# One core, macaron block with routed experts: scatters and q reads moved within the attention turn, settling merged into attention, expert weights fetched before rows

## What is computed

```python
x = x + 0.5 * ffn(_layernorm(x), waff, W1, b1, W2, b2, thr)
x = x + attn(_layernorm(x), W_qkv, u_qkv, sigma_qkv, W_proj, u_proj, sigma_proj)
x = x + 0.5 * ffn(_layernorm(x), waff, W1, b1, W2, b2, thr)
# ffn: aff = (x @ waff.T) / (|x| |waff| + 1e-9); every token goes to its best of 8 experts,
#      if its rank in its batch for that expert is < cap, where
#      cap = clip(floor(S * sigmoid(aff.mean() - thr)), 4, S); other tokens enter as zero
#      h = gelu(xi @ W1e + b1e); out += h @ W2e + b2e            (D=128, F=512, E=8)
# attn: 16 heads of 8, qkv = x @ (sigma_param / sigma * W_qkv), causal softmax, then W_proj
```

## Time and profile before

| | |
|---|---|
| runs before | 1085.56 us median of 3 (1085.16 to 1087.98) |
| profiled execution | 1081.78 us, span 1080.0 us, mean granted PE clock 0.942 |
| PE, VectorE, ACT, GpSimd busy | 904.3, 712.7, 595.9, 721.9 us |
| DMA packets | 127407, 89.72 MB, mean 83 GB/s |

### The profile page before, as it was taken

How to read it: one execution, slowest core, us unless ns; L and a number is a source line. 1 busy time by engine, 2 the same in 40 slices (tenths; PEclk the granted TensorE clock), 3 DMA queues, 4 the chain that set the end, 5 groups by cost and what they waited for, 6 DMA issues and landing times. The chain is left out here.

```text
span 1080.0 us, 26507 instructions
## 1 busy us (share of the span) xinstructions
PE 904.3 (84%) x8184; PEld 688.8 (64%) x8217; DVE 712.7 (66%) x2348; ACT 595.9 (55%) x1547; POOL 721.9 (67%) x1328
## 2 busy tenths in 40 slices
PE   5846479999747898989899999989998872899995
PEld 4733379999724555556556565556555551899995
DVE  7979734444227777878888888888888744444441
ACT  2434156666414665656666666666666550666663
POOL 6619768644035678878888898888887773255554
PEclk9999679999959999999999999999999995899998
DMA  7450022223135544354454535454544201222220
GB/s 197 121 176 0 4 60 68 68 66 66 41 86 107 106 90 98 94 98 100 97 105 96 117 96 107 100 101 96 100 107 96 53 23 38 63 68 63 66 64 20
DMA packets 127407, 89.72 MB, mean 83 GB/s; under 512 B 14305, under 2 KB 117910, under 8 KB 127270
## 3 DMA queue, kind: packets, MB, share of 16 engines
q1 hardware_dynamic: 103078, 52.69, 21.6%
q10 hardware_dynamic: 15488, 17.74, 8.1%
q0 software_dynamic: 8704, 17.60, 6.0%
HBM read 52.23 MB, written 35.47 MB: 81 GB/s over the span
## 5 line engine op out<-in xcount | busy, mean ns | idle before, releaser
L1250 ACT ACTIVATE at_pt<-at_pm 128x512 f32<-128x512 f32 x384 | 228.9, 597 | 158.9 <-PE at_pm L1336 91.7
L1558 DVE TENSOR_REDUCE at_mx<-at_pp 128x2 f32<-128x512 f32 (+1 forms) x384 | 261.7, 683 | 81.4 <-PE at_pp L1325 45.7
L1157 POOL TENSOR_SCALAR_AFFINE_SELECT at_pt<-at_pt 128x256 f32<-128x256 f32 (+1 forms) x384 | 185.7, 489 | 65.6 <-ACT at_pt L1250 61.8
L904 ACT ACTIVATE e_ht<-e_ps_h,b1t 128x128 f32<-128x128 f32 x576 | 165.0, 370 | 92.7 <-PE e_ps_h L932 92.4
L932 PE MATMUL e_ps_h<-e_xnt,e_w1own 128*128 128x128 f32 x1152 | 157.1, 281 | 3.7 <-DVE e_w1own L983 3.7
L942 PE MATMUL e_ps_y<-w,e_ht 128*128 x1152 | 159.2, 282 | 0.0
L932 PEld LDWEIGHTS e_ps_h<-e_xnt,e_w1own 128*128 128x128 f32 x1152 | 144.9, 198 | 4.2 <-issue 2.9
L942 PEld LDWEIGHTS e_ps_y<-w,e_ht 128*128 128x128 f32 x1152 | 140.0, 192 | 1.7
L989 DVE SCALAR_TENSOR_TENSOR e_y<-e_ps_y,e_x 128x256 f32<-128x256 f32 x72 | 30.6, 425 | 161.9 <-PE e_ps_y L942 161.9
L870 POOL DMA_INDIRECT out_dram<-e_y,e_x x72 | 73.9, 1027 | 93.3 <-DVE e_y L989 81.7
L1323 PE MATMUL at_pp<-kb,qs 96*128 96x512 bf16 x256 | 99.4, 388 | 14.1 <-DVE at_mx L1558 13.3
(11 more groups left out here) (322 smaller groups left out, 1776.9 us busy)
## 6 DMA issues: line engine op xcount, KB each, us to landing
at_qkd<-at_part SPq DMA_DIRECT2D x64, 192.0 KB, 2.8
kb<-at_qkd SPq DMA_DIRECT2D x64, 96.0 KB
qs<-at_qkd ACTq DMA_DIRECT2D x64, 96.0 KB
e_x<-buckets SPq DMA_DIRECT2D x72, 66.0 KB, 1.9
x<-e_y SPq DMA_DIRECT2D x36, 128.0 KB, 1.8
rows<-ts_x ACTq DMA_DIRECT2D x16, 264.0 KB, 2.8
ts_x<-in_x_dram SPq DMA_DIRECT2D x16, 256.0 KB, 3.9
x_by_token<-at_xa SPq DMA_DIRECT2D x32, 128.0 KB
```

Source lines behind the costliest of these rows:

```text
L904: last = a.activation(hid_t[j % NB][:, f, :], ps_h[j % NB][:, f, :], ACT.Gelu, bias=c.b1t[:, ds(e, 1), f])
L1157: g.affine_select(out=tile, in_=tile, compare_op=ALU.is_ge, fill=0.0, base=0, pattern=[[0, n], [1, P]], channel_multiplier=-1).then_inc(ma ...
L1250: a.activation(pt[u % RING][:, :], pm[u % 2], ACT.Exp, scale=SCALE).then_inc(exped, 1)
L1558: v.tensor_reduce(out, src, axis=AX.X, op=ALU.max).then_inc(maxed, 1)
```

## The change

In attention, the two scatters move from steps 4 and 6 to 7 and 9, the three pairs of q reads from steps 10, 11 and 1 of the next turn to 9, 10 and 11, and the gathers take their indices from `place` itself. The section `settle` becomes the end of attention's streams, with the same operations, in PSUM that attention already has. In both expert sections ACT runs a Gelu on one element first, and VectorE copies the first four weights before it waits for rows.

```diff
@@ experts
+            a.activation(early[0:1, 0:1], c.part[0:1, 0:1], ACT.Gelu).then_inc(early_done, 1)
             for i in range(-TURN, NU):
@@
             dve.wait_ge(c.w1_in, 16)
+            e = experts_of(dve, 0)
+            for j in range(FETCH):
+                fetch(j, e[j])
             for i in range(-NORM, NU):
                 if i + NORM < NU:
                     keep(i + NORM)
                 for j in (2 * i, 2 * i + 1):
-                    if 0 <= j + FETCH < NS:
+                    if FETCH <= j + FETCH < NS:
@@ attention, SP
             run(turn)
             sp.wait_ge(blanked, 16)
+            sp.wait_ge(tail_done, 1)
+            blank_tails(sp, 0)
+            sp.wait_ge(tailed, 16 * E)
             for k in range(NQ):
                 sp.wait_ge(row_out[k], 32 * (B // NQ))
@@ attention, GpSimd
+            pool.wait_ge(zeroed, NZ)
@@
-                    if u == 0 and has(4):
-                        wait(pool, xa_in[k % 2], xa_count(b + 2)(k))
-                        g.tensor_copy(index[k % 2][:, :], c.place[:, ds((b + 4) * TPB, TPB)]).then_inc(index_done, 1)
@@
-                            wait(pool, index_done, n + 1)
                         pool.indirect_dma_start(xa[k % 2][:, j, 0:D], None, x_dram,
-                                                bass.IndirectOffsetOnAxis(ap=index[k % 2][:, j:j + 1], axis=0)).then_inc(xa_in[k % 2], 16)
+                                                bass.IndirectOffsetOnAxis(ap=c.place[:, n * TPB + j:n * TPB + j + 1], axis=0)).then_inc(xa_in[k % 2], 16)
@@
-                    if u in (4, 6) and has(-4):
-                        n, j = b - 4, (u - 4) // 2
+                    if u in (7, 9) and has(-4):
+                        n, j = b - 4, (u - 7) // 2
@@ attention, ACT
-                    if u == 1 and has(2):
-                        q_rows(b + 2, (k + 2) % NQ, k % 2, 2)
@@
-                    if u in (10, 11) and has(3):
-                        q_rows(b + 3, (k + 3) % NQ, (k + 1) % 2, u - 10)
+                    if u in (9, 10, 11) and has(3):
+                        q_rows(b + 3, (k + 3) % NQ, (k + 1) % 2, u - 9)
             run(turn)
+            act.wait_ge(tail_done, 1)
+            blank_tails(act, HALF)
+            act.wait_ge(e_ask, 1)
+            a.activation(cell[:, 2:3], cell[:, 1:2], ACT.Exp, scale=-1.0).then_inc(e_got, 1)
@@ attention, PE: behind run(turn), settle's matmuls, the first of them after
+            pe.wait_ge(seen, TPB * B)
@@ attention, VectorE: behind run(turn), settle's chain, after
+            dve.wait_ge(summed, B)
```

More of the change, by code:

```diff
@@ L805, in experts @@
         y_out = [sem(f"yout{k}") for k in range(NR)]
-        fills = sem("fills")
+        fills, early_done = sem("fills"), sem("early")
+        early = t.sb(f"{tag}_early", [1, 1])
         xn_done, x_tr, x_tr_out, up, gelu, down, y_done, w1_done, kept = (
@@ L1062, in attention @@
         kept = [sem(f"kept{k}") for k in range(2)]
-        index_done = sem("index")
-        index = two("index", [P, TPB], I32)
         size, wnorm_d, tiny, far = two("size", [P, TPB]), sb("wnorm_d", [P, E]), sb("tiny", [P, TPB, E]), sb("far", [P, TPB, E], BF16)
@@ L1080, in attention, with blank_tails @@
         NM = 5
-        blk = ctx.enter_context(nc.Block())
+        cell, cols = sb("cell", [P, 8]), sb("cols", [P, 2])
+        count, tiles, tile_end, jump, ended, skipped = (sb(n, [P, E]) for n in ("count", "tiles", "end", "jump", "ended", "skipped"))
+        tail_f, tail = sb("tail_f", [1, E]), sb("tail", [1, E], I32)
+        ps_n, ps_sum, ps_row = pp[0][:, 0:E], pp[1][:, 0:1], pm[0][:, 0:2 * P]
+        settled, counted, sum_ask, sum_got, e_ask, e_got, table, rowed, tail_done, tailed = (
+            sem(n) for n in "settled counted sum_ask sum_got e_ask e_got table rowed tail tailed".split())
+        HALF = E // 2
+        blk = ctx.enter_context(nc.Block())
+        def blank_tails(eng, first):
+            _, row = nc.values_load_multi_w_load_instructions(
+                tail[0:1, first:first + HALF], engines=[eng.engine], min_val=0, max_val=E * STRIDE - P,
+                skip_runtime_bounds_check_because="a bucket of STRIDE rows holds at most T tokens, so its end leaves P rows of it")
+            for e in range(HALF):
+                eng.dma_start(io["buckets"][ds(row[e], P), :], c.blank[:, :]).then_inc(tailed, 16)
         x_t = nc.dram_tensor("x1_by_token", (T, D), F32, kind="Internal").ap()
@@ L1456, in _ @@
             run(turn)
+            pe.wait_ge(seen, TPB * B)
+            te.matmul(ps_n, c.onesb[:, :], c.hots[B % 2][:, 3 * TPB, :], start=True, stop=True).then_inc(counted, 1)
+            pe.wait_ge(sum_ask, 1)
+            te.matmul(ps_sum, c.ones[:, :], cell[:, 0:1], start=True, stop=True).then_inc(sum_got, 1)
+            pe.wait_ge(table, 1)
+            for i in range(2):
+                last = te.matmul(ps_row[0:1, i * P:(i + 1) * P], cols[:, i:i + 1], c.ident[:, :], start=True, stop=True)
+            last.then_inc(rowed, 1)
         @blk.vector
@@ L1612, in _ @@
             run(turn)
[L1615 to L1666, removed]
@@ L1667, in _ @@
+            s = Steps(dve, settled)
+            dve.wait_ge(summed, B)
             v.tensor_reduce(cell[:, 0:1], c.aff_sum[:, :, :], axis=AX.XY, op=ALU.add).then_inc(sum_ask, 1)
@@ L1683, in _ @@
             dve.wait_ge(sum_got, 1)
-            v.scalar_tensor_tensor(cell[:, 1:2], ps_sum[:, 0:1], 1.0 / (T * E), c.thr[:, :], ALU.mult, ALU.subtract).then_inc(e_ask, 1)
+            v.scalar_tensor_tensor(cell[:, 1:2], ps_sum, 1.0 / (T * E), c.thr[:, :], ALU.mult, ALU.subtract).then_inc(e_ask, 1)
             dve.wait_ge(rowed, 1)
@@ L1707, in macaron @@
         attention(nc, m, io, c, x1)
-        settle(nc, m, io, c)
         experts(nc, m, io, c, "e2", out, False)
```

## The result

The changed kernel takes 1061.03 us (median; 1059.28 to 1062.2) against 1085.57 beside it (1085.16 to 1087.98): ratio 0.977, 95% interval 0.9743 to 0.9798. That is 24.5 us where 30.5 were forecast (1085.5 to 1055). The profiled execution takes 1060.11, span 1058.4, 21.6 less than the span of before.

A forecast was written before the change was run, and what follows sets the result against it. PE was taken to set attention's pace, interrupted by late transfers. From 1081.8 us, attention 19, settling 5.9 and weights 2.6 and 1.0 (28.5) gave 1053.3, plus 1.9 gave 1055; own range 1047 to 1062, whole range 1044 to 1070.

The forecast's parts named there:

- Rival B: Attention reads stay bound by the DMA engines and k becomes the last; gain there only 5.6 us, 1068.6 total; chance 0.26.
- D: Attention: ACT waits in step 9 for landed parts, 1.54 us a turn, 37 over 24 turns; 1092 us, slower; chance 0.05.
- q's rows, 16 + 4.8: Attention: earlier q reads take 1.1 us off each PE wait, 16 in all, plus 4.8 from three low-clock turns.
- The subtraction one microsecond earlier: Attention: without step 4's scatter ahead of it, GpSimd's part subtraction L1212 goes about 1.0 us earlier, and so the parts land.
- New waits, -2: Attention: loss of 1 us for GpSimd's bunched work and 1 for waits showing once PE no longer pauses.
- rival C: Attention: GpSimd's new order delays masks and L1181, ACT waits in step 11; 10 of the 19 us lost, 1065; chance 0.13.
- Index copies, 0: GpSimd in attention: dropping one 0.18 us copy per turn gains nothing, as PE hides it; upper bound 5.8 us.
- Settling, 5.9: End of attention: with settling merged, the second experts' first load goes at 910.3 instead of 916.3, 5.9 us gained; bounds 3.5 to 7.0.
- Weights ahead of rows, 2.6 and 1.0: Experts sections: first expansion starts 2.6 us earlier in the first, 1.0 in the second, and the lead lasts.
- Early Gelu: Experts sections: moving a 1.28 us table load earlier gains nothing; up to 1.3 each if ACT were the limit.
- The added 1.9: Added to the sum: half of the 3.8 us by which the profiled execution lay below the median of the runs.

The follow-up runs named there:

- the kernel with gathers held: Changed kernel with the last four of the first 16 gathers in the first experts section held back for the first two blocks' results; 1048.31 us, ratio 0.9747 to before.

## Why the prediction came out as it did

- **Time and class.** 1061 lies inside the range and inside the forecast's own; 6 us less were saved than forecast. That it is not further off is in part luck: attention gave 5.7 us more than forecast and the first experts 8.7 less. Rival B (1068.6) asked for waits on `kb`; they fell from 3.9 to 1.5. D (1092) asked for ACT to be held in steps 9 and 10; the changed kernel's first profile shows no such wait. Its second has 2 turns, 5.6 us, and PE waits 1.2 and 1.5 us right behind them. D's step is real and rare, not in every turn.
- **q's rows, 16 + 4.8.** Forecast 19 for attention, measured 24.7 between the two profiles, 23.2 between the means of three kernels with the old attention (531.5) and six with the new (508.3). PE's wait is gone in full, not 1.1 us of each, and in the profile after no low clock is left between turns 4 and 28 (its second profile has one). The DMA share of 0.89 did not bind (0.79 in the 6.2 us from 621.5, where the changed kernel reads, and no wait of PE for q): the Trainium skill's rule in "DMA: Bandwidth & Descriptors", section on issuing engines, holds that SP's and ACT's reads share the engines, and the trace does not contradict it, but the gain came in the main from parts that land earlier, which moves all twelve reads. That is the term that was mis-sized: the prediction gave all to the read's 1.7 us of lead and nothing to the scatters, and alone they are worth 11.1 us, the reads 6.9.
- **The subtraction one microsecond earlier.** 1.4 earlier (7.98 against 9.38).
- **New waits, -2; rival C.** Too small by the trace, and more than made up by what the stalls gave back. ACT does wait for `rest_a` in step 11, as C has it, 14.9 us over 24 turns; of that 1.6 us reaches PE, not C's 10. All waits of PE for exponentials are 2.4 us in this profile, 7.9 in the second and 4.6 to 11.3 in the six others with the change, where the profile before had none (0.2 in its second); those for the maxima (`qs<-at_mt`) are 4.1, which the prediction has nowhere. From the end of the first experts to turn 0 it takes about 1 us more in most kernels with q's reads moved (50.2, 50.1, 49.3 to 50.7 against 48.3 to 49.0; the kernel with gathers held, on the other chip, has 48.9): a small loss, if it is one, that I had not looked for.
- **Index copies, 0.** Measured 2.3, not told from 0.
- **Settling, 5.9.** 5.4 between the tails of the merged kernels (43.8 on average) and of those with the scatters or reads moved (49.2); 4.4 against the kernel before. Chain and blanks went as worked out: the chain ended 5.4 us after the rank. The first load then took 2.9 us, not 1.7, and the trace has both parts of the difference. SP left its last wait for landings 0.8 us after the chain's end (892.64 after 891.81), 0.2 in settle (914.76 after 914.53). And the merged section ends by clearing attention's semaphores: GpSimd takes 0.7 us for it (893.01 to 893.71), where settle's own took 0.2 (915.11 to 915.28). The prediction took over the 1.5 to 1.7 of settle's end.
- **Weights ahead of rows, 2.6 and 1.0.** The step that failed is "both stages then run without a gap, so the lead lasts". In the first section the start moved by 2.4, and at its end 0.5 was left, which is within the spread of the profiles: the slow stretch, which ends at a set time, took the rest. In the second, which has no such stretch, 1.35 us stayed (149.35 against 150.7 on average, though the profile of before, 149.1, is as short as those with the fetch). Early Gelu: 0, as forecast.
- **The sum.** Between the two profiles 28.5 were forecast and 21.6 came. By terms, measured less forecast: attention +5.7 (24.7 against 19), tail -1.8 (4.1 against 5.9), second experts -0.9, first experts -8.7 (6.1 longer instead of 2.6 shorter), lead-in and the rest -1.1; together -6.9, by unrounded figures. The added 1.9 stood for how far timed runs lie above a profiled one; after the change that is 0.9, which gives 1.0 back. The one large term is the first experts, and 6.4 of its 8.7 are no effect of the change: the profiled execution of before lacked the slow stretch that the other profiles have (159.0 on average against 152.5). That it lay 3.8 us under the median, and below all three timed runs, was the sign; I read it as noise and added half.

## What to carry to other kernels

When a transfer is late, follow it back: the row that names the late read says nothing of how early it could be issued, and an instruction of another engine three links up, here one DMA issue ahead of a small subtraction on GpSimd, can be worth more than the issue slot (11.1 us against 6.9 here). A profiled execution outside the range of the timed runs is a warning about the base: ask what it lacks before a sum is made against it. A lead at the start of a stage is only kept if nothing later in the stage ends at a time of its own, as the slow stretch does at 17.6 to 17.9 us after the first transpose.

## What the hardware showed unexpectedly

TensorE's instructions came 0.70 us apart for 2 to 8 us in twelve of fourteen profiles (matmuls of this section otherwise follow each other at 0.11 us at the full clock). Of the two experts sections it happened only in the first, where GpSimd issues a long unbroken run of indirect DMAs. With 16 gathers it ended 17.6 to 17.9 us after the first transpose in eleven profiles (two of them have one more gap of 0.6 to 0.7 us at 18.5), with 12 at 12.2 in one. With 12 and the others held back it did not appear, in one profile on another chip.

The run of gathers is not enough by itself. TensorE kept its usual pace for at least the first 10 us after the first transpose, with the gathers going on; the first profile of before has 16 gathers and no stretch; and the ten later gathers of the last kernel slowed nothing. It starts near the same matmul (the 47th to 51st) in all, so the place in TensorE's program may have a part in it as well, though the second experts section passes that matmul without a stretch. Another rival is untried: that TensorE's own instructions came late. The trace has one transfer of 16 KB on an instruction queue (q8) near here in every profile, 10.2 us after the first transpose in the changed kernel, taking 1.1 us; but it is there at 10.6 in the kernel that has no stretch too, and at 13.1 in the first profile of before. How the gathers reach TensorE, if they do, these traces do not show.
